# A transformer block on one core: the stages from the output projection to the shared expert in one program block, sequence by sequence

## What is computed

```python
x = x + xattn(layernorm(x), ctx_1024, ctx_1024)   # 2 x 512 queries, 8192 keys, 16 heads of 32
x = x + attn(layernorm(x))                        # local attention, window of 7 keys
x = x + ffn(layernorm(x))

def attn(x):                                      # D = 512, H = 16
    q, k, v = x @ W_qkv.T + b_qkv                 # split in heads
    k_lat, v_lat = k @ W_lat.T + b_lat, v @ W_lat.T + b_lat      # per head, 32 x 32
    p = softmax(q . k_lat[window of 7] * scale)
    return (p . v_lat[window of 7]) @ W_proj.T + b_proj
def ffn(x):                                       # 1024 tokens
    scores = sigmoid(h @ gate_w.T); top 128 tokens for each of 16 experts
    out[top] += score * (silu(xin @ gw.T + gb) * (xin @ up_w.T + up_b)) @ down_w.T + down_b ...
    return out + (silu(x @ sh_gate.T) * (x @ sh_up.T)) @ sh_down.T          # shared expert, 1024 wide
```

## Time and profile before

| | us |
|---|---|
| median of 3 runs | 3174.29 (3172.49 to 3174.4) |
| the profiled execution | 3177.68 |
| its span in the trace | 3175.9 |
| end of the last cross-attention product to the first down product of expert 0 | 568.46 |

### The profile page before, as it was taken

How to read it: one execution, slowest core, us unless ns; L and a number is a source line. 1 busy time by engine, 2 the same in 40 slices (tenths; PEclk the granted TensorE clock), 3 DMA queues, 4 the chain that set the end, 5 groups by cost and what they waited for, 6 DMA issues and landing times. The chain is left out here.

```text
span 3175.9 us, 45035 instructions
## 1 busy us (share of the span) xinstructions
PE 3039.1 (96%) x15853; PEld 1820.8 (57%) x15853; DVE 1824.3 (57%) x1578; ACT 1346.5 (42%) x1871; POOL 43.9 (1%) x38
## 2 busy tenths in 40 slices
PE   8999999998999999999999997979799899999998
PEld 4888888886333333333333333358344688888886
DVE  4444444444999999999999996047244111111111
ACT  3212121222988888888888882135100011111110
POOL 0000000000000000000000000000000200000000
PEclk9999999999999999999999998976899999999999
DMA  5555555555554555544554541000330678788774
GB/s 194 185 186 191 186 193 183 197 183 181 124 132 121 126 120 124 130 121 118 122 130 120 131 120 57 0 5 1 123 159 17 226 301 314 303 311 310 303 305 179
DMA packets 231254, 518.54 MB, mean 163 GB/s; under 512 B 20578, under 2 KB 86626, under 8 KB 201436
## 3 DMA queue, kind: packets, MB, share of 16 engines
q1 hardware_dynamic: 227564, 508.74, 49.7%
q0 software_dynamic: 3584, 8.39, 1.2%
HBM read 403.62 MB, written 113.44 MB: 163 GB/s over the span
## 5 line engine op out<-in xcount | busy, mean ns | idle before, releaser
L791 DVE TENSOR_TENSOR AC<-AC,PR 128x2048 f32<-128x2048 f32 x496 | 1093.5, 2278 | 7.2 <-ACT PR L754 7.2
L754 ACT ACTIVATE PR<-PS 128x1024 f32<-128x1024 f32 x1024 | 994.4, 1023 | 144.5 <-DVE AC L791 98.2
L665 PE MATMUL PS<-QS,KS 128*128 128x512 f32 x2048 | 645.0, 436 | 19.2 <-ACTq L763 9.0
L665 PEld LDWEIGHTS PS<-QS,KS 128*128 128x128 f32 x2048 | 321.0, 189 | 549.9 <-ACT PR L754 514.4
L712 PE MATMUL PS<-PR,VC 128*32 128x512 f32 x4096 | 547.3, 606 | 1.0 <-ACT PR L754 1.0
L1393 ACT ACTIVATE SE<-PS,GB 128x128 f32<-128x128 f32 x256 | 73.2, 368 | 630.7 <-PE PS L1349 630.7
L365 ACT ACTIVATE KH<-PS,bk_s 128x512 fp32r<-128x512 f32 x128 | 88.1, 688 | 561.4 <-PE PS L416 561.4
L276 DVE SCALAR_TENSOR_TENSOR KL<-PS,bk_s,KH 128x512 fp32r<-128x512 f32 x128 | 95.8, 750 | 274.6 <-ACT KH L365 274.6
L1349 PEld LDWEIGHTS PS<-XE,WG 128*128 128x128 f32 x2048 | 238.8, 193 | 23.7 <-issue 23.7
L1349 PE MATMUL PS<-XE,WG 128*128 128x128 f32 x2048 | 240.5, 276 | 0.8 <-issue 0.8
L1349 PE MATMUL PS<-XE,WU 128*128 128x128 f32 x2048 | 239.1, 275 | 0.0
(11 more groups left out here) (149 smaller groups left out, 2265.9 us busy)
## 6 DMA issues: line engine op xcount, KB each, us to landing
KS<-kh_d SPq DMA_DIRECT2D x256, 256.0 KB
WU<-in_up_w SPq DMA_DIRECT2D x64, 1024.0 KB, 4.8
WG<-in_gw SPq DMA_DIRECT2D x64, 1024.0 KB, 6.9
WD<-in_down_w SPq DMA_DIRECT2D x64, 1024.0 KB, 8.9
AT<-in_ctx SPq DMA_DIRECT2D x32, 1024.0 KB, 5.5
kh_d<-KH SPq DMA_DIRECT2D x32, 1024.0 KB, 4.4
kl_d<-KL SPq DMA_DIRECT2D x32, 1024.0 KB, 6.4
v_d<-VS SPq DMA_DIRECT2D x128, 256.0 KB, 3.0
```

The lines of the kernel that those rows point to most:

```text
L665: m = pe.matmul(PS[:, 2 * slot + jj, :], KS[s][:, j, t * P:(t + 1) * P], QS[x_][:, j, :], start=True, stop=True)
L754: nc.scalar.activation(PR[t][:, 2 * hp:2 * hp + 2], PS[:, 2 * slot:2 * slot + 2, :], ACT.Exp, scale=SCALE).then_inc(s_exp, 1)
L791: v.tensor_tensor(a[:], a[:], PR[t][:], ALU.add).then_inc(s_acc, 1)
```

## The change

Blocks 6a, 6b, 8 and 9 become one block, and TensorE's order in it is written out by hand, one sequence a step ahead of the other.

- The first four tiles of the output projection (sequence 0, which needs no AT of the last group) move into the cross-attention block: tile 0 before the last `denominator`, tiles 1 to 3 behind it. The bias `bo` is added to X in stage 1 already, in DVE's prologue.
- PSUM banks 0 to 3 are a ring in the order of a list `ORDER` of all dense products; `claim` waits until the product four places earlier is evicted. Banks 4, 5 hold the scores of a half tile, 6, 7 its turned weights.
- The local attention runs in 20 half tiles of 8 heads. The weights are normalised before they are turned (`normal_weights`, in place), and the products with the values are swapped: the values (128 x 32) are stationary, 122 columns of turned weights move, four heads to four column groups of the array. The result has the layout that the projection wants, so the transposes L991 and the evictions L1052 and L1073 go; ACT evicts it (`values_out`). Between the half tiles stand the products of values, keys and queries (sequence 0) and the shared expert's gate and up products (sequence 1).
- LayerNorm goes by four tiles; POOL gives the inverse root (`pow`) in place of ACT's Sqrt and DVE's reciprocal.
- The shared expert runs 1024 wide for each sequence: gate and up, then down with 8 terms. Silu is written to HS, and DVE multiplies in place.
- Weights are loaded into buffers that come free inside the block, each behind a `filled(sp, ...)`. The first expert's gather is issued in this block; SP no longer waits for the stores of X at its end (POOL does, before it scatters).

```diff
                 all_groups(pe, group)
+                pe.wait_ge(s_wo, 16)
+                pe.wait_ge(s_norm, BG)
+                output_projection(pe, 0)
                 pe.wait_ge(s_acc, BG * GA + ADDS)
                 pe.wait_ge(s_rec, BG)
                 denominator(1)
+                for i in range(1, 4):
+                    output_projection(pe, i)
...
+        def claim(pe, name):
+            bank, nth = HB[name]
+            if nth:
+                pe.wait_ge(s_free[bank], nth)
+            return bank
...
+                dve.wait_ge(s_bo, 16)
+                dve.wait_ge(s_xn, TT)
+                for i in range(TT):
+                    v.tensor_tensor(X[:, i, :], X[:, i, :], BO, ALU.add)
...
+                filled(sp, "pj7")
+                sp.dma_start(SD[1][:], sh_down[:, 4:8, :]).then_inc(s_sd[1], 16)
+                for k in range(FC - 1):
+                    load_step(sp, 0, k)
...
+                    nc.gpsimd.tensor_tensor(tmp[:, q, 10], tmp[:, q, 8], minus_half[:], ALU.pow).then_inc(s_root6, 1)
...
+                def scores(b, k):
+                    t, jp = divmod(k, 2)
+                    h = b * NH + k
+                    if h:
+                        pe.wait_ge(s_wsm, h)
...
+                def turn_weights(b, k):
+                    h = b * NH + k
+                    pe.wait_ge(s_wn, h + 1)
...
+                def slot(b, k, values=None):
+                    if values is not None:
+                        window_values(b, values)
+                    if 2 <= k:
+                        turn_weights(b, k - 2)
+                    if k + 1 < NH:
+                        scores(b, k + 1)
...
+                def down(i):
+                    if i == 0:
+                        pe.wait_ge(s_sd[0], 16)
+                        pe.wait_ge(s_sd[1], 16)
...
+                slot(0, 1)
+                product("v01", WV6, XT2[0], 1)
+                slot(0, 2)
+                product("v02", WV6, XT2[0], 2)
...
+                slot(1, 4, values=0)
+                up(0, 2)
+                slot(1, 5)
+                gate(0, 3)
+                slot(1, 6, values=1)
...
+                exps(1, 4)
+                values_out(1, 0)
+                exps(1, 5)
+                silu(0, 3)
...
+                def slot(b, k):
+                    if k < NH:
+                        largest(b, k)
+                    if k >= 2:
+                        turned_out(b, k - 2)
+                    if 1 <= k <= NH:
+                        normal_weights(b, k - 1)
...
                 pool.wait_ge(s_to, 2)
-                for e in range(E):
+                for e in range(1, E):
```

More of the change, by code:

```diff
@@ new lines, in gate_logits, with gate @@
+                def gate_logits(b):
+                    bank = claim(pe, f"gate{b}")
+                    for c in range(DC):
+                        m = pe.matmul(PS[0:E, bank, :], GW[:, c, :], XT7[b][:, c, :], start=(c == 0), stop=(c == DC - 1))
+                    m.then_inc(s_full[bank], 1)
+                def gate(b, f):
+                    if b == 0 and f % 4 == 0:
+                        pe.wait_ge(s_sg[f // 4], 16)
+                    product(f"g{b}{f}", SG[f // 4], XT7[b], f % 4)
@@ new lines, in _ @@
+                slot(0, 5)
+                pe.wait_ge(s_ve, 1)
+                for t in range(NT):
+                    latent_values(0, t)
+                for t in range(NT):
+                    evicted(pe, f"vl0{t}")
+                slot(0, 6, values=0)
+                latent_keys(1, 0)
+                product("k11", WK6, XT2[1], 1)
+                slot(0, 7, values=1)
+                latent_keys(1, 1)
+                product("k12", WK6, XT2[1], 2)
+                slot(0, 8, values=2)
@@ new lines, in _ @@
+                up(0, 3)
+                slot(1, 7)
+                gate(0, 4)
+                slot(1, 8, values=2)
+                up(0, 4)
+                slot(1, 9)
+                gate(0, 5)
+                slot(1, 10, values=3)
+                up(0, 5)
+                slot(1, 11)
+                gate(0, 6)
+                window_values(1, 4)
+                up(0, 6)
+                gate(0, 7)
+                up(0, 7)
+                evicted(pe, "pv14")
+                for i in range(4, TT):
+                    projection(i)
@@ new lines, in _ @@
+                down(0)
+                down(1)
+                for i in range(4, TT):
+                    turn(3, i)
+                for i in range(4, TT):
+                    evicted(pe, f"t3{i}")
+                gate_logits(1)
+                down(2)
+                down(3)
+                for f in range(FS):
+                    gate(1, f)
+                    up(1, f)
+                down(4)
+                down(5)
+                pe.wait_ge(s_tk, 1)
+                bank = claim(pe, "topk")
@@ new lines, in gate_scores @@
+                def gate_scores(b):
+                    if b == 0:
+                        filled(act, f"vl1{NT - 1}")
+                    bank = filled(act, f"gate{b}")
+                    nc.scalar.activation(GS[0][:, b * SQ:(b + 1) * SQ], PS[0:E, bank, :], ACT.Sigmoid).then_inc(s_free[bank], 1)
+                for i in range(4):
+                    turned(2, i, XT2[0])
+                act.wait_ge(s_cst, 16 * (3 + H))
+                for g in range(G):
+                    key(0, g)
+                query(0, 0)
@@ new lines, in _ @@
+                for i in range(4, TT):
+                    turned(2, i, XT2[1])
+                for g in range(1, G):
+                    query(0, g)
+                act.wait_ge(s_wz, 1)
+                for k in range(4):
+                    exps(0, k)
+                    value(0, k)
+                exps(0, 4)
+                key(1, 0)
+                exps(0, 5)
+                exps(0, 6)
+                values_out(0, 0)
+                key(1, 1)
+                exps(0, 7)
+                values_out(0, 1)
@@ new lines, in _ @@
+                key(1, 2)
+                exps(0, 8)
+                values_out(0, 2)
+                key(1, 3)
+                exps(0, 9)
+                query(1, 0)
+                values_out(0, 3)
+                query(1, 1)
+                query(1, 2)
+                values_out(0, 4)
+                query(1, 3)
+                for g in range(G):
+                    value(1, g)
+                for i in range(4):
+                    turned(3, i, XT7[0])
+                exps(1, 0)
@@ L1229, in _ @@
+                silu(0, 5)
+                values_out(1, 3)
+                silu(0, 6)
+                values_out(1, 4)
+                silu(0, 7)
+                for i in range(4, TT):
+                    turned(3, i, XT7[1])
+                gate_scores(1)
+                for f in range(FS):
+                    silu(1, f)
             @block.vector
```

894 lines of the change are left out of this document (501 added, 393 removed).

## The result

The changed kernel takes **3062.7 us** (median of 4 runs, 3061.9 to 3063.6) where the kernel before takes 3173.6 on the same chip (4 runs, 3172.5 to 3174.4): a ratio of 0.9651, 95% interval 0.9634 to 0.9668. The forecast was 3040, its range 3018 to 3078. The direction and the range held; of the 134.6 us that the sum promised, 111 came. The result is 0.7 us over the 3062 where the prediction ended its likeliest case, and the last part says what offset what.

A forecast was written before the change was run, and what follows sets the result against it. TensorE, busy for 96% of the span, was taken to bound the kernel. Its work 380.5, idle 21.8, tiling changes 6 and end 25.6 made 433.9 us for 568.5, so 3174.3 - 134.6 = 3040 us, range 3018 to 3078.

The forecast's parts named there:

- likeliest case: Whole kernel: the forecast with the case of costlier ACT table switches included, 3020 to 3062 us; chance 67%.
- dear small forms: Half tiles: values at 3.50 us (+23), drains (+6), half tiles 0.5 us longer on DVE or ACT (+10): 3079; 15%.
- scores, 20 half tiles: Local attention scores on TensorE: 16 calls took 1.15 us, so 20 groups of 8 calls take 11.5 us.
- changes between tilings, as gaps: TensorE's about 60 changes between dense, 32-row, full and 32-column forms: nothing to 12 us, 6 us taken.
- slots set by DVE, evictions of the latent values: Sequence 0: DVE sets the first six half tiles, 0.4 us each, plus 1.7 for evictions: 4.1 us idle.
- values, swapped: Local attention value products on TensorE: 10 groups at 1.15 us, 11.5 us, up to 23 more.
- wait for SD[1], with its half rate: Before `down(0)`: 6 us idle for a late-issued 1 MB load, 2.5 us of low clock behind it, 8.5 us.
- an early wait: Rival: a bank that ACT frees late takes half of the gain, 3105 us; 5%.
- ACT's rival: Half tiles: a table switch costing 2.56 us makes ACT set the pace, 7 us over five pairs, 3047; 10%.
- Stage 1: DVE's bias additions, load landing by 88, split done at 98.1 with 3.2 us to spare: booked at nothing.
- The end: Behind the last down product: 1.5 us, then 15 gathers, 24.1 us, with TensorE waiting about 3 for DVE: 25.6 us.
- the rival at half rate: Half tiles: small groups hold the clock at 0.66, 80 us more, 3120 us; 10%.

The follow-up runs named there:

- the third series: The changed kernel rerun on another chip as base, 3069.9 us, beside ScalarE's own bias wait (3060.7), own waits and load order (3050.4) and staged gathers (3070.3).
- the first and the third series: The first: four edits of the changed kernel's constant loads or score order, 3061.8, 3049.5, 3050.3 and 3081.2 us; the changed kernel itself not run there.
- the second series: The changed kernel rerun on another chip, 3062.9 us, beside projection after denominators (3068.4), gathers in two parts (3060.7) and all edits together (3031.9).

## Why the forecast held, and where it missed

The change did what it was to do, and the clock held. But the number is in the range by offsets, and that part is luck. By the prediction's own bands 3062.7 stands at the border between the likeliest case, which ended at 3062, and "dear small forms"; and what brought it there is two costs, one that the sum did not have and one that it had at half (31 us together), less what it had booked too high elsewhere. What the sum had against what the trace has, in us, for the interval of 433.9 forecast and 454.1 measured:

| step of the sum | forecast | measured | difference |
|---|---|---|---|
| wait before the first latent key | none | 17.6 | +17.6 |
| half rate behind that wait | none | 3.0 | +3.0 |
| scores, 20 half tiles | 11.5 | 21.7 | +10.2 |
| second half tile: idle, and its products at half rate | 2.2 | 2.4 and 1.5 | +1.7 |
| eight products beside 32-row or 32-column products, 3.53 or 3.63 instead of 3.43 | none | 2.6 | +2.6 |
| changes between tilings, as gaps | 6 | 0 | -6.0 |
| slots set by DVE, evictions of the latent values | 4.1 | 1.1 | -3.0 |
| transposes of half tiles | 20.6 | 18.6 | -2.0 |
| values, swapped | 11.5 | 9.8 | -1.7 |
| wait for SD[1], with its half rate | 8.5 | 5.0 and 1.9 | -1.6 |
| latent values; transposes of tokens | 10.5; 8.2 | 9.3; 7.3 | -2.1 |
| first residual, evictions, the end | 29.4 | 28.6 | -0.8 |

The column adds up to +17.9; 2.3 us of the 20.2 are spread over the rest and stay unresolved.

**The step that failed** is one that was not in the idle list: between "1.0 us before the first key product" and "2.2 us before the second half tile" it has nothing. The sum followed buffers, banks and weights, but not what the constants' semaphore counts. The edit that moved the constants into the block's beginning put 16 small loads ahead of a wait on all of them, on ACT, whose fixed order every later eviction stands behind. Rows of the kernel before had pointed there. It has the same 16 loads (SP's timeline, then the DMA issues of 1940 to 2120 us; the last number is the median from issue to landing):

```profile
1946.24 7.83 SPq L860 DMA_DIRECT2D BLr<-in_blat_r  x16
```

```profile
BLr<-in_blat_r SPq DMA_DIRECT2D x16, 16.0 KB, 13.9
```

There too one semaphore counts all loads of the block, and all engines wait for it ahead of the QKV products. But the LayerNorm of all tiles lies between, and the first of these products starts at 1986.79, 40.5 us after the first small load was issued; 31 us are enough. In the changed kernel ACT comes to its wait at 1962.29, 7 us after the first is issued. (The 7.9 us for the mask in the earlier trace rows are another matter: one load of 305 KB that is issued only when the old local attention starts.) The rival "an early wait" had the mechanism and took it at half of the gain with 5% (half of 134.6 off 3174.3 is 3107, not its 3105); it costs 20.6 us with its half rate, 15% of the gain, and its place is ACT's first eviction, not a bank. With own waits and order the kernel takes 19.5 us less in the third series; off 3062.7 that would be about 3043, near the forecast, but this edit alone was not run without the gaps.

**The term that was mis-sized** is the scores. "16 calls took 1.15 us; 20 groups of 8 calls: 11.5 us" halves the time with the number of calls. But the old calls kept four row groups busy and the new ones keep two, so half of the instructions take nearly the same time (1.14 us for 1.15): 21.7 us in all. The run with one row group after the other shows that it is the side by side that counts. The same error hid another: DVE's half tile was priced at 5.4 us against TensorE's 5.05, so that DVE would set the first six slots; with the dearer scores TensorE needs 5.53 for such a slot (2027.09 to 2032.62), and no wait for DVE shows ahead of a half tile's transposes.

**Drains**: 6 us booked, and none shows as a gap: 2156.03 to 2159.66 to 2160.64 to 2161.62 goes through three forms without one. The cost is there all the same, in the neighbours. Eight dense products take 3.43 us among their like, 3.53 with 32-row or 32-column products on one side and 3.63 with them on both; a half tile's transposes take 0.84 between dense products and 0.93 to 0.98 beside the small ones. That is 2.6 and 1.8 us in all, 4.4 of the 6 booked, at about 0.1 us a change; the prediction's middle was near. The 12 us that it named by the rule of the Trainium skill ("TensorEngine Tiling (Array Packing)", Key Properties), that a change of mode drains TensorE, are more than this trace shows; whether the 0.1 us is such a drain, no run isolates.

**The values** at an upper bound of 3.50 us a group would have cost 23 us more; the choice of the nearer row, the cross attention's value products in four column groups, was right: 0.98 us a group to the next instruction, for 1.15.

**ACT's rival** did not come: the table load has nothing behind it.

```profile
2135.91 1.28 ACT L1291 ACT_TABLE_LOAD   x1 [4.11 <-PE PS L1071]
2137.20 0.59 ACT L1291 ACTIVATE VE<-PS 16x512 f32<-16x512 f32 x1
```

The next instruction starts 0.01 us behind the load. Some loads even run while ACT would wait anyway (2137.81 to 2139.09, with the next activation released by TensorE at 2140.57); others, like this one, start only when the wait is over. The 2.66 us of the Trainium skill ("ScalarE: Activation LUTs", What ACT_TABLE_LOAD costs) are not what a switch costs here.

**Stage 1**: the additions started at 87.70 (forecast 88) and the split was done at 97.4 (98.1), in time for 101.3; they cost nothing.

```profile
87.70 4.91 DVE L328 TENSOR_TENSOR X<-X,QQ 128x512 f32<-128x512 f32 x8 [4.20 <-DMA QQ<-in_bo]
95.16 2.28 DVE L271 TENSOR_TENSOR CL<-AT,CH 128x2048 fp32r<-128x2048 f32 x1
```

**SD[1]**: the right place, the right cause, 5.04 us of waiting for 6, and 1.9 for 2.5 of half rate. The run with split down products covers it.

**The end**: 25.4 us for 25.6, with TensorE's wait for DVE at 2.5 for 3, as "here a gain is given back" said.

**Clock**: PEclk 1.00 in both half-tile parts, so the rival at half rate fell; the half rate that is left in this interval sits behind waits of TensorE (0.60 in the 7.2 us behind the wait of 17.6; 0.88 in the 15.7 us behind that of 5.0; and the second half tile), as the sum had it for SD[1].

## What to carry to other kernels

Work moved between dense products runs at their clock, and is worth its price at that clock, not at the one it had; but for every engine with a fixed order, list what each semaphore it waits on counts, and when the last of these loads is issued, not only the buffer that the instruction reads. Price a small matmul form by a row with as many row groups side by side, not by its number of calls. Where the mode changes, look at how long the neighbours take, not only for a gap. And before a gain is called given back, run the base on the same chip: 7 us between two chips looked exactly like it.

## What the runs showed of the hardware that was not expected

- Sixteen loads of 16 KB, in pieces of 128 B, were in 31 us after the first was issued; a load of 1 MB behind them took 20.3 us instead of 8.7.
- On the chips of the first and the third series TensorE's first products of expert 0 show 5.7 to 6.4 us of gaps (0.83 ahead of the first product not counted) while a burst of 14 or 15 gathers runs, for the same kernel that shows none in its first measurement and in the second series; the burst moved, the gaps moved with it. The kernel before takes 7 to 8 us more on those chips as well; no trace shows where.
- Products of 32 rows, N = 128: 0.100 us each in one row group, 0.067 in two, 0.036 in four.
- Changes between full, 32-row and 32-column forms left no gap, but cost about 0.1 us each in the products beside them; a table load on ACT is 1.28 us with nothing behind it; `pow` over 128x4 on POOL took 1.01 to 1.04 us.
- The clock behind short waits is not the same in each execution: behind the same wait of 2.06 us the denominators took 1.95 us in one execution of the changed kernel and 2.46 in another.
